# A two-block Swin transformer on one core: transposes moved into the score-transpose banks, MLP pieces in a third bank, second MLP product one tile a step

## The reference

```
for block in (L0, L1):
    x  = x.transpose(0, 2, 3, 1)                    # tokens x 192 channels
    h  = layernorm(x)                               # folded gains in the weights
    q, k, v = windows(roll(h, -4)) @ w_qkv + b_qkv  # 12 heads of 16
    a  = softmax(q k^T / 4 [+ bias + mask])         # 64 x 64 per window and head
    x  = x + roll(unwindow((a v) @ w_proj + b), +4)
    x  = x + gelu(layernorm(x) @ w_fc1 + b1) @ w_fc2 + b2     # 192 -> 768 -> 192
    x  = x.transpose(0, 3, 1, 2)
```

## Time and profile before

| | |
|---|---|
| median of 3 runs | 4226.17 us (4218.26 to 4227.47) |
| the profiled execution: its own time | 4221.89 us |
| its span in the profile | 4220.1 us |
| granted TensorE clock over the span | 1.0 |
| TensorE matmuls busy | 92% |
| VectorE busy | 81% |
| GpSimd busy | 73% |
| ScalarE busy | 64% |

### The profile page before, as it was taken

The page is one execution under the profiler, slowest core; times in us unless marked ns, Lnnn a source line. Parts: engine busy times, 40 slices in busy tenths (PEclk is TensorE's granted clock), DMA queues, the critical chain, the costliest instruction groups (busy, mean ns, idle before and its releaser), DMA issues. The chain is left out here.

```text
span 4220.1 us, 173918 instructions
## 1 busy us (share of the span) xinstructions
PE 3900.1 (92%) x65872; PEld 2870.6 (68%) x65872; DVE 3430.2 (81%) x9093; ACT 2692.4 (64%) x5409; POOL 3085.5 (73%) x6257
## 2 busy tenths in 40 slices
PE   4999999999999999999999999999999999999998
PEld 2667667766766766766676676667666766766765
DVE  6888888888888888888888888888888888888885
ACT  1666666666666666666666666666666666666665
POOL 4777777777777777777777777777777777777775
PEclk9999999999999999999999999999999999999999
DMA  4644545445554554555546555445544555544543
GB/s 104 108 95 101 103 98 101 104 100 99 103 103 97 104 101 98 103 99 104 98 101 103 99 100 100 104 96 105 102 96 103 101 102 100 100 103 96 95 98 63
DMA packets 1545145, 421.00 MB, mean 100 GB/s; under 512 B 1441782, under 2 KB 1542522, under 8 KB 1544316
## 3 DMA queue, kind: packets, MB, share of 16 engines
q1 hardware_dynamic: 1540732, 409.87, 49.9%
q10 hardware_dynamic: 3584, 0.01, 0.0%
HBM read 32.15 MB, written 25.17 MB: 14 GB/s over the span
## 5 line engine op out<-in xcount | busy, mean ns | idle before, releaser
L968 DVE TENSOR_TENSOR hid<-scaled,hid 128x512 f16<-128x512 f32 x768 | 674.1, 891 | 344.9 <-POOL hid L1137 325.5
L600 PE MATMUL bank<-w_fc,hid 128*128 128x192 f16 x9216 | 845.4, 246 | 106.9 <-DVE hid L968 104.8
L587 PE MATMUL ps_s<-xh,w_fc 128*128 128x512 f16 x3840 | 859.2, 379 | 70.9 <-ACT stage L709 64.5
L1074 POOL TENSOR_TENSOR rstd<-vare,half 128x2 f32<-128x2 f32 x520 | 360.6, 693 | 770.1 <-DVE vare L908 770.1
L600 PEld LDWEIGHTS bank<-w_fc,hid 128*128 128x128 f16 x9216 | 761.4, 98 | 195.9 <-DVE v_blk L924 169.6
L587 PEld LDWEIGHTS ps_s<-xh,w_fc 128*128 128x128 f16 x3840 | 355.5, 97 | 560.5 <-issue 110.9
L1137 POOL TENSOR_SCALAR hid<-scaled 128x512 f16<-128x512 f32 x768 | 564.7, 739 | 121.8 <-ACT scaled L723 120.9
L723 ACT ACTIVATE scaled<-ps_s,b_fc 128x512 f32<-128x512 f32 x768 | 529.3, 689 | 154.5 <-PE ps_s L587 133.7
L690 ACT ACTIVATE xs<-xn 128x192 f16<-128x192 f32 x512 | 185.7, 363 | 683.2 <-POOL xn L1081 683.2
L715 ACT ACTIVATE pt<-ps_t 128x768 f16<-128x768 f32 x512 | 415.7, 812 | 303.8 <-PE ps_t L544 300.7
L463 PE MATMUL bank<-w_qkv,xh 128*128 128x384 f16 x2560 | 501.0, 326 | 6.1 <-DMA xh<-xs 3.6
(11 more groups left out here) (113 smaller groups left out, 7182.7 us busy)
## 6 DMA issues: line engine op xcount, KB each, us to landing
x_img<-in_x_dram SPq DMA_DIRECT2D x256, 96.0 KB, 2.2
out_dram<-y_img SPq DMA_DIRECT2D x256, 96.0 KB, 2.0
xh<-xs SPq DMA_TRANSPOSE x520, 2.5
qkt<-qk SPq DMA_TRANSPOSE x512, 3.3
ot<-os SPq DMA_TRANSPOSE x512, 2.3
stage<-in_L_conv_fc_w_dram SPq DMA_DIRECT2D x2, 384.0 KB, 4.3
stage<-in_L_conv_w_fc_dram SPq DMA_DIRECT2D x2, 384.0 KB, 4.2
stage<-in_L_conv_qkv_w_dram SPq DMA_DIRECT2D x2, 288.0 KB
```

The costliest lines, as they stand in the source:

```text
L587: last = mm(ps_s[:, u % 2, :].rearrange("p (a t) -> p a t", a=GROUP), w_fc1[layer][:, part, m * 128:(m + 1) * 128], xh[:, p % 2 * GROUP:(p ...
L600: mm(bank[:, 0:C], hid16[:, hs, m, tok], w_fc2[layer][:, ws, m, :], start=(m == 0 and i == 0), stop=False)
L968: v.tensor_tensor(hid16[:, 1, m, :], hid[:, u % 4, :], hid16[:, 0, m, :], ALU.subtract)\
```

## The change

It does six things.

1. The x transposes write bank 0 of `ps_t` and the y transposes bank 1. Both wait for `p_lo` of visit s-2, the last reader of P there, and `p_transpose` waits for both copies out. All stand at the start of a step; y comes two steps after `mlp_out`.
2. The bank that this frees (`ps_hid`) takes pieces 0 and 5; pieces 1 to 4 stay in the score banks. Pieces 0 to 3 still stand at the end of place 0, pieces 4 and 5 at the start of place 1.
3. `mlp_out(s-10)` stands at the end of every step's scores and q/k product, always in `ps_v`: tile 0 at place 2, tile 1 at place 3, tiles 2 and 3 at places 0 and 1 of the next phase. In place 0 it stands ahead of `hidden(0)`. The split pieces get a second buffer.
4. VectorE's order is new: `mlp_residual` first, pieces 0 to 4 split at the start of place 1, piece 5 inside place 2, `statistics` and both `mean_variance` after `v_lo`.
5. ScalarE does gelu 2 to 5 at the start of place 1 without a break, GpSimd splits piece 4 first there.
6. Groups of block 0 and block 1 change places in the table.

```diff
+OUT = LATE + 2
-        order += [(image - 2, 1, 0), (image, 0, 0), (image - 2, 1, 1), (image, 0, 1)]
+        order += [(image, 0, 0), (image - 2, 1, 0), (image, 0, 1), (image - 2, 1, 1)]
-        ps_tr, ps_o, ps_qk, ps_v = banks
+        ps_hid, ps_o, ps_qk, ps_v = banks
+        hid_banks = [ps_hid[:, :], ps_s[:, 0, :], ps_s[:, 1, :], ps_s[:, 0, :], ps_s[:, 1, :], ps_hid[:, :]]
+        ps_x = ps_t[:, 0, 0:C]
+        ps_y = ps_t[0:H2, 1, 0:2 * TOK].rearrange("p (k t) -> p k t", k=2)
...
                 def x_transpose(n):
-                    take_tr("x_in", rank(n))
+                    ge("p_lo", min(n - 8, ENDS))
+                    ge("x_in", rank(n) - 1)
...
                 def v_product(n):
-                    if place == 1 or p < 0 or p == 0 == place:
+                    if n <= OUT:
                         ge("v_lo", n - 1)
                     else:
-                        ge("resid2", p * GROUP + (-1, None, 0, 2)[place])
+                        ge("resid2", n - OUT - 1)
...
                 def hidden(m):
+                        ge("gelu", u - 1)
+                    if m == 1:
                         ge("exp_done", min(s, ENDS))
-                    if m >= 2:
-                        ge("gelu", u - 2)
+                    if m >= 3:
+                        ge("gelu", u - (2, 2, 5)[m - 3])
...
+                if live(s - OUT):
+                    mlp_out(s - OUT)
                 if mlp and place == 0:
-                    for m in range(3):
+                    for m in range(4):
                         hidden(m)
-                if mlp and place > 0:
-                    ge("v_lo", min(s, ENDS))
-                    mlp_out(p * GROUP + (0, 0, 2, 3)[place], ps_v)
...
                 mlp = 0 <= p < PHASES
+                if live(s - OUT - 1):
+                    mlp_residual(s - OUT - 1)
                 if mlp and place == 1:
-                    hidden_lo(2)
-                    hidden_lo(3)
+                    for m in range(5):
+                        hidden_lo(m)
...
+                if mlp and place == 1 and live(s - 1):
+                    p_lo(s - 1)
+                if mlp and place == 2:
                     hidden_lo(5)
                 if live(s - 3):
+                    statistics(s - 3, 1)
+                if live(s + 5):
+                    mean_variance(s + 5, 0)
```

More of the change, by code:

```diff
@@ L406, in slot @@
                     load(visit(s + 9)[0] + 1, visit(s + 9)[2])
[L407 to L410, removed]
+                n = s - OUT - 4
+                if live(n) and visit(n)[1] == 1:
+                    ge("y_ready", rank(n) | 1)
+                    store(visit(n)[0], visit(n)[2])
             run(slot)
@@ L505, in rel_scores @@
                     if place == 1:
-                        ge("gelu", p * HC + HC - 1)
+                        ge("gelu", p * HC + 4)
                     ge("exp_done", n - 1)
@@ L541, in p_transpose @@
                     ge("p_lo", n - 1)
+                    if live(s + 6) and visit(s + 6)[1] == 0:
+                        ge("x_in", rank(s + 6))
+                    if live(s - OUT - 2) and visit(s - OUT - 2)[1] == 1:
+                        ge("y_ready", rank(s - OUT - 2))
                     ge("exp_done", n)
@@ L548, in pv_product @@
                 def pv_product(n):
[L551 to L554, removed]
+                    ge("o_norm", n - 1)
                     ge("v_lo", n)
@@ L590, in hidden, with mlp_out @@
                     last.then_inc(S["fc1"], 1)
-                def mlp_out(n, bank):
+                def mlp_out(n):
                     _, layer, t = visit(n)
@@ L619, in slot @@
                     x_transpose(s + 6)
-                if live(s) and place != 1:
+                if live(s - OUT - 2) and visit(s - OUT - 2)[1] == 1:
+                    y_transpose(s - OUT - 2)
+                if live(s):
                     rel_scores(s)
@@ L625, in slot @@
                     v_product(s)
-                if live(s) and place == 1:
-                    rel_scores(s)
-                if live(s):
                     scores(s)
@@ L633, in slot @@
                     p_transpose(s - 1)
-                if place == 1 and live(s - LATE - 2) and visit(s - LATE - 2)[1] == 1:
-                    y_transpose(s - LATE - 2)
-                if mlp and place == 2:
-                    if visit(p * GROUP)[1] == 1:
-                        y_transpose(p * GROUP)
-                    ge("o_norm", min(s - 2, ENDS))
-                    mlp_out(p * GROUP + 1, ps_o)
-                if mlp and place == 3 and visit(p * GROUP)[1] == 1:
-                    y_transpose(p * GROUP + 2)
                 if live(s):
@@ L742, in y_evac @@
                             act.wait_ge(y_stored[h], 16 * image)
-                    tile = ps_tr[0:H2, 0:2 * TOK].rearrange("p (k t) -> p k t", k=2)
-                    for win, img in box_pairs(t, tile, y_img[:, :, :]):
+                    for win, img in box_pairs(t, ps_y, y_img[:, :, :]):
                         last = copy(img, win, ACT.Copy)
@@ L776, in slot @@
                     load_gelu()
-                    gelu(0)
                 if live(s + 3):
@@ L780, in slot @@
                 if mlp and place == 0:
+                    gelu(0)
                     gelu(1)
-                if last_block and place == 2:
-                    y_evac(p * GROUP + 1)
             run(slot)
@@ L959, in attention_residual, with mlp_residual @@
                     residual(n, ps_qk[:, 0:C], stream(n, 1), stream(n, 0), "pr", "resid1")
-                def mlp_residual(n, bank):
-                    residual(n, bank[:, 0:C], token_rows(n), stream(n, 1), "fc2", "resid2")
+                def mlp_residual(n):
+                    residual(n, ps_v[:, 0:C], token_rows(n), stream(n, 1), "fc2", "resid2")
                 def hidden_lo(m):
@@ L1141, in slot @@
                 mlp = 0 <= p < PHASES
+                if mlp and place == 1:
+                    hidden_hi(4)
                 if live(s + 4):
@@ L1149, in slot @@
                     set_mask(s + 3)
-                if mlp and place == 1:
-                    hidden_hi(5)
                 if live(s - 2):
```

83 lines of the change are left out of this document (28 added, 55 removed).

## The result

The changed kernel takes **4255.44 us** (median of 4 runs, 4254.22 to 4257.32), the kernel before, beside it, 4224.76 (4218.26 to 4227.47). The ratio is 1.0075, 95% interval 1.0058 to 1.0093. The forecast was 4211, 15 us won; 31 were lost. The time lies in the range 4115 to 4310, but it moved the other way. The profiled execution has 4257.32 us and a span of 4255.5.

A forecast was written before the change was run, and what follows sets the result against it. TensorE was busy 92%, with VectorE a close second bound through their common chain. Phases of 31.67 and 32.03 us gained 0.16 on average, 20 us over 126; less 4 and 1, 4207 profiled, 4211 median; range 4115 to 4310.

The forecast's parts named there:

- closed loop through `ps_v`: Plain step: v_product waits for mlp_residual in the same bank, so VectorE sets the step at 5.94 us.
- the late hi copy of v: Place 2 to 3: ScalarE's hi copy of v comes late by an estimated 0.19 us, between nothing and 0.4.
- the second term: Place 2 to 3, block-1 phase: loop 5.94 plus piece 5 at 0.72 plus 0.19, making 6.85 us against 7.40.
- Rival A: TensorE's waits for exp and pieces come from a bank shortage and go: 4057 us, smaller form 4135; chance 0.15.
- the plain step: Step without MLP pieces: as long as before, 5.94 us, set by VectorE; 5.5 us would show the forecast wrong.
- the sum's term for place 0 to 1: From row_max of place 0 to that of place 1: 9.35 to gelu 4 plus 3.35, 12.70 us against 12.16.
- the upper bound of 3.61: Place 0 to 1, gelu 4 to row_max: the old kernel's time; the lower bound, an unhindered chain, was 2.75 us.
- the first 40 steps: Steps ahead of the first phase: x and bias lose about 0.4 us in ten steps, 4 us.
- the last steps and the end: Kernel's end: residuals of the last four tiles come one after the other as before; 1 us put.
- a new wait for a DMA: Sign of being wrong: such a wait, since GpSimd's normalisations in place 1 come later than before; no size given.
- Rival B: Place 1: the pieces' chain sets the phase, deciding from 12.9 us for 0 to 1; 4287 us, chance 0.30.

The follow-up runs named there:

- e1: Changed kernel with VectorE's input statistics moved from the end of a step to behind mlp_residual at the next step's start; 4228.33 us, ratio 1.0011.
- e4: Changed kernel with hidden(0) made to wait for exp again, although it has its own bank; 4255.10 us, ratio 1.0080.
- e7: Changed kernel with GpSimd's mask copy in place 1 set between the copy of piece 4 and the norm subtraction; 4232.95 us, ratio 1.0021.
- e8: Changed kernel with the split of piece 5 moved to the start of place 2, ahead of the reciprocal; 4203.47 us, ratio 0.9952.
- e3: Changed kernel with the bias product ahead of the x and y transposes; 4221.74 us, ratio 0.9998.
- e5: Changed kernel with the split of piece 4 in place 1 moved from ahead of row_max to behind v_lo; 4344.60 us, ratio 1.0287.
- e9: Changed kernel with the edits of e2, e3, e7 and e8 together; 4136.13 us, ratio 0.9795.
- e2: Changed kernel with mlp_residual ahead of qk_lo in the same step instead of at the next step's start; 4220.91 us, ratio 0.9995.
- e10: e9 with the attention output's transpose earlier in place 1, on GpSimd and in SP's queue; 4131.71 us, ratio 0.9785.
- e6: Changed kernel with place 0's mlp_out moved behind pieces 4 and 5, its residual behind the split pieces; 4293.62 us, ratio 1.0166.

## Why the prediction was wrong

The view of the kernel held in the main. VectorE and TensorE share a closed loop through `ps_v` (e1); `hidden(0)` starts 3.74 after `row_max` (said: 3.71), gelu 4 at 9.34 (9.35), and of the eight intervals four came within 0.04 (6.09, 7.30, 5.98 in phase 0, 6.18 in phase 1) and one, 5.84, 0.10 under the forecast. The 7.30 is luck in part: the split of piece 5 cost more than was put and the late hi copy of v less, as the second term below shows. Rival A falls: the wait for exp went and no time with it, and the plain step stayed near 5.9. By the Trainium skill's reading of a repeating gap ("Perfetto Trace Analysis", Optimization Strategy) too little PSUM was one possible cause. In the new order it isn't what holds piece 0, since with the wait for exp put back (e4) the time is 4255.10 against 4255.44; of the old order no run tells.

**The step that failed is the sum's term for place 0 to 1**: "I take 3.35" from gelu 4 to `row_max`. It measured 3.56 (12.90 - 9.34), between 3.35 and the upper bound of 3.61. The prediction had taken the lower value because the copy of piece 4 no longer stood behind a subtraction on GpSimd. True, but the subtraction now starts just ahead of the *split* of piece 4, which takes 0.96 instead of 0.69. e7 shows it: with these two in the other order, 0.26 of the interval go. By means (12.92) the term is 0.22 a phase too small. Against the kernel before the interval grew by 0.73: `hidden(0)` starts 0.77 later (0.74 said), and from gelu 4 to `row_max` only 0.05 was won (0.26 said).

**The second term is 2 to 3 of phase 1**: 6.85 said, 7.17 measured (mean 7.22). The prediction put piece 5 on VectorE's loop at 0.72 and the late hi copy of v at 0.19, together 0.91. In the trace `p_lo` starts 4.12 after `row_max` in place 2 of phase 1 and 2.92 in place 3 (medians), 1.20 later. Of this 0.90 is the split (0.98 less the 0.08 by which neighbours overlap), and 0.30 is `v_lo`, which starts at 1.44 instead of 1.14 because it waits for the hi copy. So the two costs were the right ones, and both were taken too small. In phase 0 `v_lo` is only 0.04 late and `p_lo` 0.95: there 0.18 too little and 0.15 too much cancel, and the interval comes out at 7.30 (7.29 said). That `mlp_out` would still wait for piece 5 the prediction had wrong, but this wait doesn't set the step: behind `mlp_out` TensorE waits for `p_lo` again, in 54 of 55 phases 1 (P·V) and in all of phases 0 (x transposes). By means the term is 0.37 too small in every other phase, 0.18 a phase. e8 takes 0.43 from that interval by moving the split; what the hi copy would give if it came in time, no run shows.

The account is made against the forecast's 4207 for a profiled execution; it had 4257.32, 50 us more. In the 110 steady phases the two terms make 0.40, the other intervals add up to 0.01, and the phases of before were 0.06 longer by their means than the one of each kind that the prediction added up. That is 0.35 a phase, 39 us. The other 11 lie at the ends: the first 40 steps lose 7.2 us where about 4 were said (x transposes ahead of the bias product: e3 gives back 5.9, of which some may be chance), and the last steps and the end lose 3 + 3 where 1 was said. What makes those 6 us was not tried. One of the waits for the attention output's transpose stands there, 4.1 us, where before it was 1.8.

These waits are of the kind that the prediction named as a sign of being wrong, a new wait for a DMA: 24.4 us in 34 waits against 1.8 in one. In the steady part it hardly counts: the interval 2 to 3 is 0.05 (phase 0) and 0.09 (phase 1) longer on average in the 28 places 2 that have it, about 2 us in all.

Rival B had the right place, and 12.90 is its point of decision. But its mechanism was only half there: the pieces do alternate with GpSimd, while the table load behind the gelus holds nothing up in place 1 as long as `row_max` is this late (it does in e5). Its price was twice the loss, 61 us over the kernel before against 31. So the outcome lies between forecast and rival: a sum of terms of 0.5 us with opposite signs, whose net of 0.16 a phase was smaller than the distance between the bounds of one of them (12.10 to 12.96).

What e9 adds: the change's parts are not bad in themselves. With the same banks, the same `mlp_out` order and the same number of instructions, four places in VectorE's, GpSimd's and TensorE's order decide between 0.75% slower and 2.1% faster. What bounds the plain step of 5.57 in e1 and e2 was not tried by itself.

## What to carry to other kernels

When two engines run a closed loop, price every moved instruction by where it stands: ahead of a wait that the engine has anyway it costs little (piece 5 in e8), between the wait's end and the loop's last link its whole length and more (piece 4 in e5). Where a forecast's net is smaller than the bounds of one term, that term deserves the work: ask which instruction of the other engine starts next to it. The largest wait of a profile need not be on the path, as e10 shows; make it go away and look at the marks.

## What was unexpected of the hardware

Two instructions of 0.55 and 0.69 us on GpSimd and VectorE that meet take either 0.55 and 0.96 or 1.04 and 0.69, decided by a start 0.14 earlier or 0.05 later: an order on one engine sets the duration on another. Copies and splits of a piece that run back to back stretch in the same way (copy 0.62 to 1.16). And the table load of 1.28 us on ScalarE is hidden behind `mlp_out` in the changed kernel, but appears at once when the hidden pieces start 1.57 earlier (e6): gelu 0 then starts 1.4 us after its piece is ready. The second load, behind the gelus, appears in the same way when `row_max` comes 0.5 to 0.9 earlier (e5): `v_lo` waits 0.20 to 0.42.
